# A four-layer graph network on one core: the third layer's head sums written straight into node tiles, four weight buffers in the first layer's narrow chunks, and a reordered last step of the fourth layer

## What is computed

```
x = layernorm(x + L0(x, adj))   # 3-head sign attention + two GRU cells
x = layernorm(x + L1(x, adj))   # D^-1/2 adj D^-1/2 x W^T + b
x = layernorm(x + L2(x, adj))   # GAT, 2 heads of 128
x = layernorm(x + L3(x, adj))   # GAT, 4 heads of 64, mask adj > 0.5
```

```
adj = adj + eye(n)
xt = einsum('nf,hfo->hno', x, W)              # (2, N, 128)
e1, e2 = a1 . xt, a2 . xt                     # (2, N)
scores = leaky_relu(e1[:, :, None] + e2[:, None, :], 0.2)
attn = softmax(where(adj > 0, scores, -9e15), axis=-1)
h_prime = einsum('hij,hjo->hio', attn, xt)    # (2, N, 128)
return elu(h_prime.reshape(n, 256))
```

## Time and profile before

| | us |
|---|---|
| median of 3 runs (lowest to highest) | 2177.42 (2175.49 to 2177.68) |
| the profiled execution's own time | 2175.57 |
| its span, first to last instruction | 2173.9 |
| PE busy | 2064.6 (95%) |
| DVE busy | 1549.1 (71%) |
| ACT busy | 963.2 (44%) |
| POOL busy | 132.2 (6%) |
| mean granted TensorE clock | 0.977 |

### The profile page before, as it was taken

One profiled execution on the slowest core, in us unless ns is written; L12 is line 12 of the kernel. 1 busy time (PEld: TensorE's weight loads), 2 busy tenths in 40 slices (PEclk: granted clock), 3 DMA queues, 4 the chain that ended last, 5 costly groups with the idle time before them and its releaser, 6 DMA issues.

```text
span 2173.9 us, 28504 instructions
## 1 busy us (share of the span) xinstructions
PE 2064.6 (95%) x10803; PEld 1159.6 (53%) x10803; DVE 1549.1 (71%) x2621; ACT 963.2 (44%) x1505; POOL 132.2 (6%) x169
## 2 busy tenths in 40 slices
PE   7999999899999999999999999999999978999996
PEld 4556665344444455555555534557999953333242
DVE  4665557797978875443778853444899956989997
ACT  3222226798888877664222210002121246644442
POOL 0000000000000000000001010000010040002011
PEclk9999999899999999999999999999999989999997
DMA  7665645455555554742000034541100115332231
GB/s 232 217 213 190 202 141 201 172 205 189 177 180 194 198 165 160 230 139 95 0 1 0 0 103 127 132 130 45 51 23 20 39 41 187 103 94 87 80 89 34
DMA packets 133176, 265.69 MB, mean 122 GB/s; under 512 B 15258, under 2 KB 62904, under 8 KB 130200
## 3 DMA queue, kind: packets, MB, share of 16 engines
q1 hardware_dynamic: 114712, 234.50, 34.0%
q10 hardware_dynamic: 18324, 29.34, 3.6%
HBM read 220.43 MB, written 43.36 MB: 121 GB/s over the span
## 4 chain that ended last, share of the span: by engine, by line
PE 64%; DVE 23%; ACT 8%; issue 4%; DMA 1%; POOL 0%; DVEq 0%; SPq 0%; ACTq 0%; POOLq 0%
PE banks L1051 20%; PE banks L954 9%; PE banks L1102 9%; PE banks L1136 6%; DVE arena L2116 5%; PE banks L1164 5%; PE banks L943 3%; DVE arena L2043 3%; PE banks L1177 3%; ACT arena L1286 2%; PE banks L995 2%; PE banks L861 2%; DVE arena L1687 2%; DVE arena L1770 1%; DVE arena L1871 1%
## 5 line engine op out<-in xcount | busy, mean ns | idle before, releaser
L1051 PE MATMUL banks<-arena 128*128 128x512 f32 (+2 forms) x1512 | 588.4, 548 | 19.4 <-DVE arena L1770 19.2
L1051 PEld LDWEIGHTS banks<-arena 128*128 128x128 f32 x1512 | 285.4, 191 | 312.2 <-issue 234.8
L1770 DVE TENSOR_TENSOR arena<-arena 128x1536 f32<-128x1536 f32 (+4 forms) x132 | 201.6, 1527 | 157.8 <-ACT arena L1322 150.4
L2116 DVE SCALAR_TENSOR_TENSOR arena<-arena 128x1024 f32<-128x1024 f32 (+3 forms) x264 | 293.1, 1181 | 16.0 <-PE banks L1177 13.2
L1164 PE MATMUL banks<-arena 128*32 128x512 f32 (+3 forms) x2112 | 221.3, 555 | 13.5 <-DVE arena L2116 13.5
L954 PE MATMUL banks<-arena 128*128 128x512 f32 (+4 forms) x528 | 222.5, 543 | 0.2 <-ACT arena L1227 0.2
L1136 PE MATMUL banks<-arena 128*124 128x129 f32 (+2 forms) x1936 | 217.7, 274 | 4.0 <-DVE arena L2043 3.3
L1136 PEld LDWEIGHTS banks<-arena 128*124 128x124 f32 (+2 forms) x1936 | 214.6, 186 | 7.3 <-DVE arena L2043 4.8
L1102 PE MATMUL banks<-arena 128*128 128x512 f32 (+4 forms) x528 | 207.7, 547 | 5.1 <-DVE arena L1872 3.7
L1315 ACT ACTIVATE arena<-arena 128x512 f32<-128x512 f32 (+4 forms) x264 | 162.8, 662 | 82.7 <-PE banks L1051 76.5
L1687 DVE CUSTOM_DVE_ANT_0 arena<-arena 128x2708 f32<-128x2708 bf16 (+1 forms) x66 | 196.2, 2973 | 1.6 <-DMA arena<-e_rows 1.3
(11 more groups left out here) (224 smaller groups left out, 2236.4 us busy)
## 6 DMA issues: line engine op xcount, KB each, us to landing
arena<-hw_rows SPq DMA_DIRECT2D x126, 384.0 KB, 3.1
arena<-adj_T SPq DMA_DIRECT2D x126, 256.0 KB, 3.2
arena<-in_adj SPq DMA_DIRECT2D x17, 1354.0 KB
arena<-in_adj SPq DMA_DIRECT2D x42, 512.0 KB
adj_T<-arena ACTq DMA_DIRECT2D x63, 256.0 KB, 2.3
arena<-adj_T SPq DMA_DIRECT2D x84, 192.0 KB, 3.0
arena<-in_adj SPq DMA_DIRECT2D x15, 1024.0 KB
arena<-in_adj SPq DMA_DIRECT2D x15, 768.0 KB
```

The source lines that it names most:

```text
L1051: ins = PE.matmul(bank(2 * (c % 2) + f)[:, 0:wid(c)], hs[0:R, m % 3, h * D + f * P:h * D + (f + 1) * P], E[0:R, n % 3, h, 0:wid(c)], start ...
L1770: V.tensor_tensor(e, e, a, ALU.mult).then_inc(s["p_ok"], 1)
L2116: V.scalar_tensor_tensor(PM3[0:k, n % 3, h, 0:w], r3_bc[0:k, h, c * WW:c * WW + w], smalls[0:k, 4, h * T + t:h * T + t + 1], mask3[0:k, n ...
```

## The change

Three things are changed.

1. **Third layer.** A tile of sums is now a tile of 128 rows of the result (`BLOCKS`, `pieces2`): for tile t PE multiplies the even nodes' columns and the odd nodes' columns of one head (`head2`), 128 columns each, and both land side by side in the same partitions. `mask2` and the factor row `r2_bc` hold even nodes in one half and odd nodes in the other; the mask steps of the second layer write them so, and the factor rows are transposed with a reordered identity. PM2 is one instruction of 2 x 512 elements per unit in place of two of 496. Tile 10 has 74 rows of head 0 and 54 of head 1, which come from two blocks and are put together at the end (`mixed`); in the last chunk PM2 takes two instructions, of 2 x 148 and 2 x 54. The trip through `heads2` is gone with its 2 waits per chunk; ACT's scaling by the divisors is merged into the ELU's own steps (`negative_part`, `positive_part`, with `nd2` and `dd2`). ELU additions stand two units apart from t = 9, normalizations one per unit from t = 18, and what is left for the projection is three tiles' ELU and seven tiles' normalization. PE waits before the projection for the last but one chunk's sums to be read, no longer for the last one's.
2. **First layer.** In the narrow chunks the same memory is cut into four weight buffers (`E_narrow`), and ACT and DVE wait there for unit n - 4. Rows of tiles 18 to 21 move by up to two units, and the shifts start at unit t = 16, 14, 12, 12 and 6 of chunks 0 to 4 (`SHIFTS_AT`), not at t = 16 of each, with store and load one unit apart on SP.
3. **Fourth layer's last unit and what follows.** The last unit does the divisor rows first. ACT copies each third of PSUM once its rows are ready; the divisors of all six tiles are transposed together between the two feature steps; DVE then multiplies and adds straight out of PSUM (`last_terms`), 64 columns at a time, and POOL does only the last pair's term for empty columns.

```diff
+EVEN = N // 2
...
+BLOCKS = [[c * RPC + r for r in range(min(RPC, T - 1 - c * RPC))] for c in range(CH)]
+BLOCKS[CH - 1].append(T - 1)
...
+def pieces2(c):
+    lo, hi = BLOCKS[c][0] * R, min((BLOCKS[c][-1] + 1) * R, N)
+    if c == CH - 1:
+        return [(1, lo - EVEN, N - lo, 0), (1, 0, R - FIRST_OF_1, N - lo + R - TAIL - (R - FIRST_OF_1))]
+    if hi <= EVEN:
+        return [(0, lo, hi - lo, 0)]
+    if lo >= EVEN:
+        return [(1, lo - EVEN, hi - lo, 0)]
+    return [(0, lo, EVEN - lo, 0), (1, (MIXED + 1) * R - EVEN, hi - (MIXED + 1) * R, (MIXED + 1) * R - lo)]
...
+def head2(t):
+    return 0 if t <= MIXED else 1
...
-           14: (46, 47, 48, 49), 15: (50, 51, 52, 54), 16: (55, 56, 57, 58), 17: (59, 60, 61, 62), 18: (64, 65, 66, 67),
-           19: (69, 70, 72, 74), 20: (76, 77, 79, 81), 21: (83, 84, 86, 88)}
+           14: (46, 47, 48, 49), 15: (50, 51, 52, 54), 16: (55, 56, 57, 58), 17: (59, 60, 61, 62), 18: (64, 65, 67, 69),
+           19: (71, 72, 74, 76), 20: (78, 79, 81, 83), 21: (85, 86, 88, 90)}
...
+        def weights_of(n):
+            if n in NARROW:
+                return E_narrow[:, (n - NARROW[0]) % 4]
+            return E[:, (n if n < NARROW[0] else n - NARROW[-1] - 1) % 3]
+        def weights_free(eng, n):
+            if n >= 3:
+                eng.wait_ge(sw["C"]["mm_done"], n - 3 if n in NARROW[3:] else n - 2)
...
+            if k == "r2":
+                for h in range(heads):
+                    load(sp, dram[h].rearrange("q (t i) -> t q i", t=T), rows_s[h * T:(h + 1) * T, 0:R].rearrange(
+                        "t (q i) -> t q i", q=2), rows[k][3])
+                sp.wait_ge(rows[k][3], 16 * heads)
+                load(sp, bc[:, 0, :, 0:W], dram[0, :, 0:W].partition_broadcast(P), rows[k][4])
+                load(sp, bc[:, 0, :, W:EVEN], dram[0, :, W:EVEN].partition_broadcast(P), rest_bc[k])
+                load(sp, bc[:, 1], dram[1, :, 0:EVEN].partition_broadcast(P), rest_bc[k])
...
-                    maxima_row(sp, c + 1)
+                if n - 4 in SHIFTS:
+                    maxima_stored(sp, SHIFTS[n - 4])
+                if n - 5 in SHIFTS:
+                    maxima_spread(sp, SHIFTS[n - 5])
...
-            for c in range(CH):
-                sp.wait_ge(l2_heads, H2 * sum(len(blocks2(i)) for i in range(c + 1)))
-                full = sum(nr == R2 for nr in blocks2(c))
...
+            order = ident.rearrange("p (i q) -> p q i", q=2) if k == "r2" else ident[:, :]
+            out = bank(b)[0:heads * T, 0:P]
+            PE.transpose(out.rearrange("p (q i) -> p q i", q=2) if k == "r2" else out, src, order).then_inc(rows[k][1], 1)
...
                     if c >= 2:
                         pe.wait_ge(l2_read, c - 1)
                     begun = set()
-                for h in range(H2):
-                    pe.wait_ge(l2_p, n * H2 + h + 1)
-                    for r, nr in enumerate(blocks2(c)):
-                        k = r * H2 + h
-                        ins = PE.matmul(bank(b0 + k // 3)[0:nr, (k % 3) * (C2 + 1):(k % 3 + 1) * (C2 + 1)],
-                                        PM2[0:kp(t), n % 3, h, r * R2:r * R2 + nr], proj2[0:kp(t), t, h, :],
+                pe.wait_ge(l2_p, n + 1)
+                for r, g in enumerate(BLOCKS[c]):
+                    for q in range(2):
+                        k = 2 * r + q
+                        ins = PE.matmul(bank(b0 + k // 3)[:, (k % 3) * (C2 + 1):(k % 3 + 1) * (C2 + 1)],
+                                        PM2[0:kp(t), n % 3, q, r * R:(r + 1) * R], proj2[0:kp(t), t, head2(g), :],
                                         start=k // 3 not in begun, stop=t == T - 1, skip_group_check=True)
                         begun.add(k // 3)
                 ins.then_inc(l2_mm, 1)
-            pe.wait_ge(l2_read, CH)
+            pe.wait_ge(l2_read, CH - 1)
...
-                backs(v)
+            degrees(UNITS3 - 1).then_inc(l3_mm, 1)
+            features(UNITS3 - 1, 0)
+            pe.wait_ge(fin_scaled, LAST[0])
+            pe.wait_ge(l3_read, RAW3 * (CW - 1) + 1)
+            for i, g in enumerate(LAST_TILES):
+                ins = PE.transpose(bank(6, 2)[:, i * P:(i + 1) * P], rawT3[:, 2, g % DT * R:(g % DT + 1) * R], ident)
+            ins.then_inc(tail_ps, 1)
+            features(UNITS3 - 1, 2)
+            for k in range(RAW3 - 1):
+                pe.wait_ge(l3_read, RAW3 * (CW - 1) + k + 2)
+                for g in LAST_TILES:
+                    ins = PE.transpose(turned_back(g)[:, k * P:(k + 1) * P], rawT3[:, k, g % DT * R:(g % DT + 1) * R], ident)
+                    if k and g % 2:
+                        ins.then_inc(tail_ps, 1)
...
+            def negative_part(c, r, t):
+                for q in range(2):
+                    ins = S.activation(tmp2[:, t, half(q)], tmp[:, t, half(q)], ACT.Relu, scale=scale_of(c, r, q, nd2))
+                ins.then_inc(elu_neg, 1)
...
-                    S.activation(tmp[0:kp(t), k, :], tmp[0:kp(t), k, :], ACT.Exp, scale=-1.0).then_inc(elu_exp, 1)
+                whole = [(r, t) for r, t in enumerate(BLOCKS[c]) if t in BATCH[c]]
+                for r, t in whole:
+                    negative_part(c, r, t)
+                if MIXED in BLOCKS[c]:
+                    r = BLOCKS[c].index(MIXED)
+                    for q in range(2):
+                        S.activation(tmp2[:, MIXED, half(q)], tmp[:, MIXED, half(q)], ACT.Copy, scale=scale_of(c, r, q, dd2))
+                act.wait_ge(elu_neg, batch_end(c))
+                for r, t in whole:
+                    positive_part(c, r, t)
+                act.wait_ge(elu_pos, batch_end(c))
...
+            def whole_scaled():
+                act.wait_ge(l2_read, CH)
+                for q in range(2):
+                    ins = S.activation(tmp[:, T - 1, half(q)], tmp[:, T - 1, half(q)], ACT.Copy, scale=scale_of(LASTC, MR, q, dd2))
+                ins.then_inc(l2_heads, 1)
...
                     roots_2(c)
-            act_project(act, 2, {2: lambda: roots_2(CH - 2), 6: lambda: elus(CH - 1), 12: lambda: roots_2(CH - 1)})
+            act_project(act, 2, {1: whole_scaled, 2: last_negative, 4: mixed_negative, 5: last_positive, 6: last_exponentials,
+                                 8: lambda: roots_2(CH - 2), 13: lambda: roots_2(CH - 1)})
...
-                m = mask2[0:k, t, col(c):col(c) + w]
-                ins = V.tensor_scalar(m, strip, 0.0, None, ALU.is_gt)
+                m = mask2[0:k, t, :, col(c) // 2:(col(c) + w) // 2]
+                ins = V.tensor_scalar(m.rearrange("p q i -> p i q"), strip.rearrange("p (i q) -> p i q", q=2), 0.0, None, ALU.is_gt)
...
+                V.tensor_scalar(nd2, dd2, -1.0, None, ALU.mult)
+            def tile_sums(c, r):
+                b0, t = 3 * (c % 2), BLOCKS[c][r]
+                f = slice(head2(t) * C2, (head2(t) + 1) * C2)
+                for q in range(2):
+                    k = 2 * r + q
+                    ins = V.scalar_tensor_tensor(tmp[:, t, q * C2:(q + 1) * C2], sum_bc[:, f], zz2[:, k // 3, k % 3:k % 3 + 1],
+                                                 bank(b0 + k // 3)[:, (k % 3) * (C2 + 1):(k % 3) * (C2 + 1) + C2],
+                                                 ALU.mult, ALU.add)
...
-                    if 13 <= t < 13 + hi - lo:
-                        ins = elu_added(lo + t - 13)
-                        if lo + t - 13 == hi - 1:
-                            link(ins)
-                            variances_2(c - 1)
-                    if t == T - 1:
-                        batch_normed(c - 1)
-            sums_out(CH - 1)
...
+                for h, lo, w, at in pieces2(c):
+                    ins = V.scalar_tensor_tensor(PM2[0:k, n % 3, :, at:at + w], r2_bc[0:k, h, :, lo:lo + w],
+                                                 smalls[0:k, 4, h * T + t:h * T + t + 1], mask2[0:k, t, :, lo:lo + w],
+                                                 ALU.max, ALU.mult)
+                ins.then_inc(l2_p, 1)
+                if c == 0:
+                    continue
+                lo, hi = batch_end(c - 2), batch_end(c - 1)
+                if t == 2:
+                    divisors_2(c - 1)
+                if 2 <= t < 2 + len(BLOCKS[c - 1]):
+                    tile_sums(c - 1, t - 2)
+                i, odd = divmod(t - (9 if c < CH - 1 else 13), 2)
+                if i in range(hi - lo) and not odd:
+                    ins = elu_added(lo + i)
+                    if lo + i == hi - 1:
+                        link(ins)
+                        variances_2(c - 1)
+                if c < CH - 1 and t >= 18 and t - 18 < hi - lo:
+                    batch_normed(c - 1, slice(t - 18, t - 17))
...
             dve_project(dve, 2, ((proj3, 0, 0, D + 2 * H3),), {
-                1: lambda: batch_added(CH - 2), 4: lambda: batch_normed(CH - 2),
-                9: lambda: batch_added(CH - 1), 13: lambda: batch_normed(CH - 1)})
```

(23 more changed lines are left out.)

327 lines of the change are left out of this document (180 added, 147 removed).

## The result

| | before | after |
|---|---|---|
| median of 4 runs, us | 2176.45 | 2158.84 |
| lowest to highest | 2172.89 to 2177.68 | 2157.58 to 2165.79 |
| ratio after / before, 95% interval | | 0.9922 [0.9907, 0.9937] |

The account below looks back on a forecast made before the run. PE, busy 95%, bounds the kernel; gains come from its idle or lower-clock stretches or DVE work setting its pace. Terms -7.7 +0.9 +1.0 -2.0 +1.1 -18.7 -4.5 sum to -29.9, giving 2147 us, range 2138 to 2160.

Parts of the forecast that it names:

- First layer: First layer's sweep: earlier shifts, spread row table and fourth weight buffer save 7.7 us, bounds 3.2 and 10.7.
- rival B: Narrow chunks: the fourth buffer does nothing, first layer gains only 3.2, total 2151.5; counted inside the forecast's 0.62.
- The loop without PE: First layer's narrow chunk 3: waits go round DVE's `row_head`, ACT and DVE's `weighted`; 4.5 us a chunk stay lost.
- Masks: Second layer's mask steps, output hopping by half a row: +0.9 us, four exposed steps at 0.22; bounds 0 and 2.5.
- Rival C: Second layer: DVE's mask steps become the bound, a step of 1.95 us cancels the gain; 2211 at 2.2; chance 0.03.
- Start of the third layer: Before the third layer's products: second store and longer first PM2 cost 1.0 us, bounds 0.5 and 3.
- Chunks 0 to 4: Third layer: all 2.0 us of PE idle time goes, the time of one product stays; -2.0, bounds 0 and -2.0.
- Chunk 5: Third layer's last chunk: DVE as late as PE, 23.3 us, +1.1; bounds 0 and +4.5.
- Projection: Projection after the third layer: 48.67 us falls to 30.0 without memory trip and low clock, -18.7; bounds -22 and -9.
- Rival A: Projection keeps its lower clock or its chain of waits: 38.5 us, +8.5, total 2156 (2152 to 2162); chance 0.17.
- the tail: After the fourth layer's last unit: DVE alone adds straight from PSUM; -4.5 us, bounds -3 and -6.
- Rival D: No stall in projection and narrow chunks (-22, -10.7), tail -6: total 2136 (2133 to 2141); chance 0.12.

Follow-up runs that it names:

- the repeat: The changed kernel, unaltered, run and profiled again beside the experiments: median 2160.12 us of five runs, ratio to before 0.9933; profiled execution 2159.47 us.

## Why the prediction promised 12 us too much, step by step

Measured against the profile of the repeat, which is nearest to the median.

**First layer: right in size, wrong in one cause.** -6.5 for -7.7. The load of `m_rows` no longer holds unit 44: chunks 0 to 2 gained 0.2 + 2.0 + 1.5 from start to start (3.2 forecast). Chunk 3 gained 3.2 (94.3, just above the 91 to 94 of the forecast), chunk 4 lost 0.3, 2.9 for 4.5. I had written that the fourth buffer lets DVE run ahead over the bias steps. It does not; rival B was right on the buffer and wrong on the gain, which was the table's. The loop without PE of the earlier trace rows runs on, with PE idle 0.58 us again and again in chunk 3.

**Masks: the step that failed.** +11.4 for +0.9. Both factors were too small. The price: I took 0.22 us more a step from copies whose *source* had a stride, with 4-byte elements; a strided *output* of bytes costs 0.81 more. (I also read 399 ns as the price of 512 elements; it is the mean over all sizes, and 512 took 438.) The trace of before had no such output, and the page "Vector Engine (DVE) Microarchitecture Reference" of the Trainium skill ("Measured stream behaviour on trn2") had spoken against it with 1.71 ns a column, an estimate of 0.95 us for 512; measured is 1.33, or 2.6 ns a column, above even that (the page's figure is for 4-byte words). So where the page and the nearest row differed, the row was the wrong neighbour, since it differed from the new instruction in which side hops. The cover: with DVE's idle time of 97 us I held all but four steps for hidden. The three in the gates are exposed as forecast, at 0.9 us each and not 0.22: +3.1. The other +8.3 are the sweep. There the program lets PE wait for DVE only in the 22 units whose own tile lies in the chunk, since DVE must add to the strip's diagonal (L1963), and this addition stands behind the mask step. PE waits at ten places where it waited for DVE at two, one of them the sweep's start, and at all others for L1963; in the repeat these waits sum to 5.8 us within the sweep, against 1.2. The rest of the 8.3 is not split further. The upper bound, 2.5 us ("each three times as dear"), tripled the price of four steps only, and never asked how many would be exposed at that price. Rival C had the sign, with a threshold of 1.95 us for losing it all, but its mechanism was DVE as the bound of every unit, and DVE still idles 26.8 us; between "hidden" and "the bound" there was a middle that I left out: 11 of the 107 us that the steps grew by (132 x 0.81) reached the time.

**Start of the third layer: right**, +1.0 for +1.0. PE's wait for the first PM2 is 1.56 for 0.59.

**Chunks 0 to 4: the gaps went, the product grew.** -0.4 for -2.0. The idle time of 2.0 us went (198.52 busy of 198.52). With 124 loaded columns the five chunks take 195.7, 3.2 less than before, so a little more than the shown idle time went. "So does the time of one" was wrong: 0.53 us a chunk for 128 loaded columns instead of 124, 2.9 us between the two runs' five chunks. Before, all loads were of 124 or 104 columns, at which the runs show no price of the load, and I carried their time past it.

**Chunk 5: right in its mechanism, too small.** +2.3 for +1.1, 24.5 us for 23.3. DVE sets the pace, as forecast: it is busy for 22.4 us, for a sum of 21.4, or 23 beside POOL, and PM2 does take 833 ns instead of 526 beside POOL's additions. What I left out is that PE's last products come behind DVE's last step: that ends at 1754.02, the products at 1755.64. Two additions fewer make the chunk 1.5 us shorter.

**Projection: right**, -18.4 (-17.3) for -18.7, with pauses of at most 1.74 us, and a clock of 1.00 (0.95). Of its stalls none was measured by itself, and its terms add up to 30.2, not 30.0. Rival A is out: the clock came back.

**Fourth layer: the tail right, a gain elsewhere not seen.** -7.1 for -4.5. Of the 7.1 about 4 are the tail. In after's last 18 us the chain is DVE's, as forecast: 16 steps for the empty-column terms from 2146.27 to 2150.78, three pairs of 1.62 plus statistics. The 16 took 0.28 us each and not 0.19, the first eight 0.35, while POOL works on its terms (2145.76 to 2148.61); the later ones from PSUM 0.20. What I had not seen are the two waits of 1.1 us at the chunk boundaries, where the same edit of `chunk_out` lets ACT copy the features before the divisor rows end; with what follows them they are the other 3.

```profile
2146.27 4.51 DVE L2241 SCALAR_TENSOR_TENSOR arena<-arena 128x64 f32<-128x64 f32 x16
...
2150.82 1.63 DVE L2241 SCALAR_TENSOR_TENSOR arena<-banks,arena 128x64 f32<-128x64 f32 x8
```

Together: in the profiled executions the repeat is 13.8 us above the forecast. The masks are 10.5 of them, the untouched first stage 3.4, and the errors of the other stages (+1.2 first layer, +2.9 third, +0.3 projection, -2.6 fourth, -1.9 ahead of it) nearly cancel, which is luck. The medians are 11.3 above (2158.8 for 2147.5), and with the masks mended the kernel takes 2148.3.

That the time lies inside 2138 to 2160 is luck too. It is there because the range had taken in most of rival A (2152 to 2162), and A did not happen; no rival had a loss of 11 us in the masks. (Rival D's terms add up to 2139.7, not 2136; it did not come in any case.)

## What to carry to other kernels

Price a new instruction by a row that has the stride on the same side and the same element size; if the trace has none, a written price for a hop on that side is a better end of the range than a row with the hop on the other. Where DVE's waits hide a step, look for the units in which PE waits for something that stands behind it in DVE's program, and count those at the upper price. Cut stretches of two kernels at the same product, and check the cut by the number of records. When one order of elements makes one side hop, try the other order first: here it is one line and 12 us.

## What the runs showed of the hardware

- A one-byte output that hops by 1354 bytes at each element costs 1333 ns for 512 elements; by 8 bytes 837; by 2 bytes 433; in a row, with the input hopping by 8 bytes instead, 457; with no hop on either side, 438.
- Products over 129 moving fp32 columns come at the same pace within 0.3% with 64, 120 and 124 loaded columns (39.04 to 39.15 us a chunk) and 1.4% slower with 128 (39.68).
- A PM2 step of DVE over 296 fp32 elements, with two inputs in SBUF, took 526 ns alone and 833 beside additions of POOL.
- A pause of PE of about 1.5 us in the same place was followed by a granted clock of 0.85 over 11 us in four executions and of 1.00 in eight, and the four are 1.6 us longer there. So part of what executions differ by is the clock after equal pauses.
